# A graph network on one core: the least number of edge batches per half is two lower, and one round's first one-hots stand behind its batch

## What is computed

```python
msg = f(x[src])                               # a row per edge
agg = segment_sum(msg, dst, n_nodes)          # sum of the edges' rows by destination
out = dense(agg, x)                           # small matrix products, norm, relu
```

## Time and profile before

| | |
|---|---|
| median of 3 runs | 5534.78 us (5533.51 to 5537.9) |
| the profiled execution | 5538.54 us, of which the span from first to last instruction is 5536.7 us |
| PE busy | 4431.4 us, 80% |
| DVE busy | 3431.3 us, 62% |
| ACT busy | 2420.0 us, 44% |
| POOL busy | 1939.0 us, 35% |
| mean granted TensorE clock | 0.931 of full speed |

### The profile page before, as it was taken

The page is one execution under the profiler, slowest core; times in us unless marked ns, Lnnn a source line. Parts: engine busy times, 40 slices in busy tenths (PEclk is TensorE's granted clock), DMA queues, the critical chain, the costliest instruction groups (busy, mean ns, idle before and its releaser), DMA issues.

```text
span 5536.7 us, 129573 instructions
## 1 busy us (share of the span) xinstructions
PE 4431.4 (80%) x25128; PEld 2900.1 (52%) x25129; DVE 3431.3 (62%) x10510; ACT 2420.0 (44%) x4967; POOL 1939.0 (35%) x1886
## 2 busy tenths in 40 slices
PE   6998897666868888867777578787699996888885
PEld 3664554333435555534554245554477773776762
DVE  5553453667545555446887488886566663777774
ACT  2542342444347777534665266664222221233332
POOL 5741781653043333007550344410333320433310
PEclk9999999899879999988999799999899999999998
DMA  4663784555334444325553266653344433344332
GB/s 129 220 203 117 236 270 146 169 180 174 102 104 141 145 143 140 117 90 151 167 167 123 93 193 199 204 185 129 118 132 137 141 120 125 112 125 126 122 112 86
DMA packets 443919, 815.61 MB, mean 147 GB/s; under 512 B 70872, under 2 KB 76818, under 8 KB 443828
## 3 DMA queue, kind: packets, MB, share of 16 engines
q1 hardware_dynamic: 389172, 697.28, 37.4%
q0 software_dynamic: 54656, 117.32, 8.6%
HBM read 480.10 MB, written 334.22 MB: 147 GB/s over the span
## 4 chain that ended last, share of the span: by engine, by line
PE 44%; DVE 16%; issue 14%; POOL 7%; DVEq 7%; ACT 5%; DMA 4%; ACTq 2%; SPq 1%; POOLq 0%
PE p_edge L1102 7%; PE p_agg L1115 7%; PE p_agg L1117 6%; POOL raw L679 6%; PE p_tr L1102 5%; PE p_agg L1148 4%; DVE onehot L1549 3%; DVE stats L1638 3%; DMA h_in<-feature 2%; PE p_wide L1179 2%; ACT o L880 2%; PE p_dense L1191 2%; PE p_wide L1235 2%; DVE u L1677 2%; DVEq L371 2%
## 5 line engine op out<-in xcount | busy, mean ns | idle before, releaser
L1549 DVE TENSOR_SCALAR onehot<-iota,dst_f,negbase 128x512 f16<-128x512 f16 (+1 forms) x2848 | 1104.8, 442 | 901.3 <-issue 335.0
L1115 PE MATMUL p_agg<-onehot,msg 128*128 128x512 f16 (+1 forms) x2848 | 1147.2, 403 | 626.3 <-DVE onehot L1549 409.1
L679 POOL DMA_INDIRECT raw<-node_s,src_i x980 | 978.6, 999 | 1567.8 <-DMA node_s<-o 667.1
L1117 PE MATMUL p_agg<-onehot,msg 128*128 128x512 f16 (+1 forms) x2848 | 1149.5, 404 | 0.0
L1115 PEld LDWEIGHTS p_agg<-onehot,msg 128*128 x2848 | 284.2, 100 | 964.5 <-issue 812.8
L679 POOL DMA_INDIRECT raw<-node_x,src_i x392 | 378.4, 965 | 629.0 <-DMA feature<-more_masked 294.9
L880 ACT ACTIVATE o<-v_ring,nmr,rstd 128x128 f32 (+1 forms) x1176 | 472.4, 482 | 61.0 <-DVE nmr L1654 56.3
L1148 PE MATMUL p_agg<-h_in,w 128*128 128x512 f32 x784 | 443.3, 649 | 56.8 <-DMA h_in<-feature 54.7
L1638 DVE BATCH_NORM_STATS2 stats<-v_ring 128x6 f32 (+1 forms) x1960 | 417.1, 279 | 63.7 <-DVE v_ring L1628 22.0
L1117 PEld LDWEIGHTS p_agg<-onehot,msg 128*128 x2848 | 284.7, 100 | 226.9 <-issue 42.5
L899 ACT ACTIVATE u<-v_ring,nmr,rstd 128x128 f32 (+1 forms) x784 | 312.5, 480 | 205.8 <-DVE nmr L1654 143.5
(11 more groups left out here) (260 smaller groups left out, 7834.4 us busy)
## 6 DMA issues: line engine op xcount, KB each, us to landing
node_s<-o SPq DMA_DIRECT2D x392, 256.0 KB
h_in<-feature SPq DMA_DIRECT2D x392, 256.0 KB
feature<-u SPq DMA_DIRECT2D x294, 256.0 KB
node_x<-o SPq DMA_DIRECT2D x294, 256.0 KB
res_in<-node_x SPq DMA_DIRECT2D x294, 256.0 KB
h_in<-node_s SPq DMA_DIRECT2D x196, 256.0 KB
h_t<-dinv_scratch SPq DMA_DIRECT2D x196, 256.0 KB
h_in<-in_x SPq DMA_DIRECT2D x98, 256.0 KB
```

What stands on the lines that cost most here:

```text
L679: nc.gpsimd.indirect_dma_start(out=raw[:, (e % RING) * BATCH + j, :], out_offset=None, in_=src_d, in_offset=bass.IndirectOffsetOnAxis(ap=s ...
L1115: nc.tensor.matmul(p_agg[:, a, :], tile_ap(msg, t, 0, D), oh, start=first, stop=True, skip_group_check=True)
L1117: return nc.tensor.matmul(p_agg[:, a, :], tile_ap(msg, t, D, 2 * D), oh, start=False, stop=True, skip_group_check=True)
L1549: return V.tensor_scalar(tile_ap(onehot, slot), iota[:, :], dst_f[:, bass.ds(t, 1)], negbase[:, bass.ds(it * 2 + a, 1)], ALU.subtract, ALU ...
```

## The change

The lower bound on the batches of a half goes from h/3 + 0.5 to h/3 - 1.5 (what the tiles need stays). And in GIN, `first_onehots` of the next pair's half 0 leaves its place ahead of DVE's batch and is issued in `onehots`, behind the batch and behind `more_onehots` of the present pair; in RGCN it stays.

```diff
+LATER = 2
...
-            link(V.tensor_scalar(some, rowf[g, :], 1.0 / 3.0, 0.5, ALU.mult, ALU.add))
+            link(V.tensor_scalar(some, rowf[g, :], 1.0 / 3.0, 0.5 - LATER, ALU.mult, ALU.add))
...
                     if rel or k == 3:
                         these, (now, after) = odd_list(dve, PT, it * 2 + 1)
-                        first_onehots(it + 1, 0, after[0])
+                        if rel:
+                            first_onehots(it + 1, 0, after[0])
                         each_batch(dve, *these, batch)
...
                 def onehots(it, these):
 
-                    if not (rel or k == 3):
+                    if not rel:
                         first_onehots(it, 0, these[0])
                     more_onehots(it, 0, these)
```

## The result

The changed kernel takes 5441.91 us (median, 5431.22 to 5450.81), the one before, in the same comparison, 5536.34 us; the ratio is 0.9827, with a 95% interval of 0.9806 to 0.9848. So 94 us are gone where 68 were forecast. Medians in this document leave out three executions, one of groups_first (10252 us) and two of groups_batch (5664.8 and 6861.3 us), which took far longer than all others for a reason that stays open. The profiled execution went from a span of 5536.7 to 5437.2 us, 99.5 us less, and PE's busy time from 4431.4 to 4393.5 us with the same 25128 products.

The account below looks back on a forecast made before the run. It took early ACT waits for POOL, POOL's pace in round 2 and PE in rounds 7 and 8 as bounds; 61 us (bound) plus 7 (one-hots) gave 68, 5467 us; range 5448 to 5487, with rivals 5445 to 5503.

Parts of the forecast that it names:

- What bounds a start: First four pairs of rounds 1, 2, 3, 5, 6: ACT waits for POOL on batches no running tile needs.
- Round 1: Bound's gain in round 1: 45.5 - 34.7 = 11 at the first four pairs, taken as 10 us.
- round 5: Bound's gain in round 5: 51.6 - 41 = 10 at the start, less 2 in the tail, 8 us.
- round 6: Bound's gain in round 6: 60.1 - 46 = 14 at the start, less 3 for the tail, 11 us.
- Round 2: Batch 25 comes when it came but belongs to step 38, not 35; gain 20 us.
- Three pairs shorter: Round 2's tail after batch 25 runs as before with three pairs fewer, which take 21 us.
- 14 if the first pairs stay 6 us slow: Condition on round 2's 20 us: only 14 if its first pairs remain 6 us slow.
- Round 3: Bound's gain in round 3: 50.5 - 42.0 = 8.5 at the start, tail 1 us worse, 8 us.
- Round 4's bound: Two batches out at round 4's start, two in at its tail: 0 us, bounds -5 and +5.
- Round 4's one-hots: Moving them behind the batch starts the low part's chain 1.1 us sooner, PE's products later; gain 7 us.
- Some 0.6 us for three pairs, 13 times: Round 4's one-hot gain: the second batch step's PE wait of 2.58 us for ACT shrinks; 7 us in all.
- Rounds 7 and 8: PE-bound; two batches of 11.8 us out at the start, two in at the tail; gain 2 us each.

Follow-up runs that it names:

- groups_first: Changed kernel, but round 4's order is groups of the present half 1, fixed one-hots of the next half 0, batch: 5454.31 us.
- groups_batch: Changed kernel, but round 4's order is groups of the present half 1, batch, fixed one-hots of the next half 0: 5433.2 us.
- later_1: Changed kernel with the bound lower by one batch in place of two, h/3 - 0.5: 5445.98 us.
- hots_only: Changed kernel with the old bound h/3 + 0.5; only round 4's fixed one-hots stand behind the batch: 5517.79 us.
- tail_only: Changed kernel, but the bound is h/3 + 0.5 up to half 60, stands still to half 66, then h/3 - 1.5: 5512.22 us.
- start_smooth: Changed kernel, but the bound is the smaller of h/3 + 0.5 and h/2 - 3.75, late only at the start: 5448.05 us.
- bound_only: Changed kernel without the one-hots' move in round 4, so the bound h/3 - 1.5 alone: 5457.55 us.
- hots_between: Changed kernel, but round 4's fixed one-hots stand inside the batch, between its low part and embedded sum: 5468.76 us.

## Why the prediction was wrong, point by point

**What bounds a start: right.** ACT waiting for POOL on batches that no tile needed was the cause of the slow first pairs. Every kernel with the late start lost that stretch (later_1 already), and hots_only and tail_only, without it, kept 45.6 to 60.1 us there.

**Round 1 (10, measured 12.3), round 5 (8, 11.6), round 6 (11, 13.4): right, each a little small.** I priced unstalled pairs from pair 1 of round 6, 9.4 us. In the kernel after, pairs 1 of rounds 5 and 6 take 7.2 us each, and round 1's pair 0 takes 7.2 us where the steady pace is 8.7. The first four pairs of rounds 5 and 6 take 38.4 and 43.2 us; I had 41 and 46.

**Round 2 (20, measured 19.3): right.** POOL's pace carries the end of the round: batch 25 comes 269.5 us after the first product before and 269.6 after, and three pairs fewer are left behind it. "Three pairs shorter" is no gain of its own: the lead alone gave 2.1 us (tail_only), the short start alone 0.9 (start_smooth), both together 19.3. The prediction had this as a condition, "14 if the first pairs stay 6 us slow"; the expectations after it forgot that.

**Round 3 (8, measured 16.9): a term mis-sized.** The step "50.5 - 42.0 = 8.5" priced the first four pairs at the middle's pace, which I did not do for rounds 5 and 6. They take 35.0 us: the first pairs of a round have no statistics and norm of earlier pairs to do. In six middle pairs of the kernel before DVE is busy 44.7 us, 29.8 for four, and in the first four of the kernel after 22.6. The stretch gave 15.5 us; the rest up to 16.9 is within the spread.

**Round 4's bound (0): right**, 2.7 us, 9.1 won at the start and 7.6 lost in pairs 40 to 47.

**Round 4's one-hots (7, measured 19 beside the bound and 21 alone): the step that failed.** The step put the whole gain on a shorter wait of PE, 0.6 us for three pairs, and put PE's busy time and the groups at nothing. I followed one chain right: the low part and the sum start sooner, PE's products start later (PE's new wait of 1.90 us in the first step, 1.7 forecast), and the wait for ACT covers it. "Some 0.6 us for three pairs, 13 times" then missed two things. In the middle three pairs went from 51.1 us on average, between 49.9 and 53.0, to 49.7 or 49.8 every time: 1.3 us. But PE's idle time fell by only 1.6 us in the ten times three pairs, where the step makes it 6; the other 11.6 us are products that were shorter in sum, at a granted clock of 0.99 for 0.96. And in pairs 40 to 47 the same move took three one-hots from ahead of the groups that PE needs first; I had taken the order of the groups for no part of the change, though the diff shows that `first_onehots` is moved past `more_onehots` too. hots_only shows 9.5 us for it, and the table of orders separates it from the move behind the batch: 4.3 us beside the new bound. What sets the middle's time stays open in part. The shorter DVE instructions (below) do not set it: in groups_batch those 30 take 49.4 us where they take 45.3 in the changed kernel, and the 30 pairs 497.5 against 497.6. Whether the chain came first and the clock followed, or the clock made the gain, was not separated. The step's arithmetic was off too, without changing the outcome: 13 times 0.6 us is 7.8 and not 7, and 26 times 1.1 is 28.6 and not 25.

**Rounds 7 and 8 (2 and 2, measured 0.5 and 3.2): right.** Two batches out, two in: 26.2 us less in the first four pairs of round 7, 25.8 more in pairs 40 to 47 (76.8 to 102.6).

**The range.** It was made of halved distances, on the ground that the ends will not meet; with the whole distances, 107 us of gain, the measured 94 would have lain inside. But rounds 3 and 4 were both mis-sized downwards, and the terms of rounds 1, 5 and 6 leaned the same way for the same reason: steady pairs are no measure of first pairs. Rounds 1, 3, 5 and 6 together came out 17 us above the forecast, round 4's one-hots 12 to 14.

## What to carry to other kernels

In this kernel, work that an in-order engine took in ahead of its need cost little in the middle of most rounds, and the supplier's latency at the start: look at the first steps of each loop by themselves, and price them by what they would hold without the wait, not by the steady pace. Where a piece is moved in one engine's order, write down every piece that it passes, and ask for each who waits for it and when; here the gain passed by unnoticed stood in eight pairs out of 49. A lead over a slow supplier paid only where the engines arrived early enough to use it, and work that is caught up two pieces to a step can cost more than it saved.

## What the runs showed of the hardware that was not expected

One long wait of PE went with a lower clock than two short ones. In pairs 6 to 35 of round 4, with waits for ACT of 3.1 to 3.5 us at the longest, the granted clock was 0.96 before, 0.95 in bound_only and in hots_between and 0.93 in groups_first; with waits of 2.4 us at most for the one-hots and 1.1 us for ACT it was 0.99 in the changed kernel and in hots_only and 1.00 in groups_batch, although the waits' sum, 56 us in the changed kernel against 59 before, and all of PE's idle time, 74.5 against 76.1, are nearly the same. The same work, some 2180 products, took PE 423 us in place of 435. That the length of a wait is the cause is only suggested by the kernels falling on two sides; it was not tried by itself.

The second is a DVE instruction of round 4, the product of rows and `dinv` with two inputs in SBUF, its durations (min/median/max in ns, first and last start), before:

```profile
L1751 DVE TENSOR_TENSOR u<-o,dinv x49: 1190/1444/2355, 1627.8 to 2471.7; 128x1024 f32<-128x1024 f32 x49
```

and after:

```profile
L1753 DVE TENSOR_TENSOR u<-o,dinv x49: 1194/1227/1825, 1570.8 to 2400.6; 128x1024 f32<-128x1024 f32 x49
```

Half of them run in steps with a batch: 26 before and 24 after overlap POOL's multiplication of that batch (L709 before, 1.68 us long), and each of these is longer by nearly what is left of POOL's instruction when it starts; the others take 1.19 to 1.23 us. Before, most began 0.42 us after POOL's and took 2.34 us; in the changed kernel DVE reaches them later, 1.11 us after POOL's, and they take 1.65. The whole median falls by 0.2 us, the longest by 0.5. The Trainium skill (SBUF — State Buffer, section "SBUF: two separate sides") says that a DVE instruction with two SBUF inputs and a GpSimd instruction that reads SBUF lock each other out of a shared port pair; this trace agrees, with 2.3 us at the longest against 1.2 us at the shortest. The same rule's other half, by which denser one-hots would have held round 2's gathers, did not show: its gathers kept 0.94 us each and 0.30 us between them.
